# Query parts of the first layer's last piece stacked through DRAM, and every large transfer in pieces on SP's queue

## What is computed

```python
def _L0_xattn_ref(x1, x2, Wq, bq, Wk, bk, Wv, bv, Wo, bo):
    q = _split_heads(x1 @ Wq.T + bq, HEADS)
    k = _split_heads(x2 @ Wk.T + bk, HEADS)
    v = _split_heads(x2 @ Wv.T + bv, HEADS)
    scores = jnp.einsum('bhqd,bhkd->bhqk', q, k) / jnp.sqrt(jnp.float32(dh))
    attn = jax.nn.softmax(scores, axis=-1)
    out = jnp.einsum('bhqk,bhkd->bhqd', attn, v)
    ...
```

## Time and profile before

| | us |
|---|---|
| median of 3 runs (207.86 to 208.6) | 208.3 |
| the profiled execution, its own time | 209.72 |
| its span, first to last instruction | 207.6 |
| PE busy in the span | 192.6 (93%), 1,447 matmuls |
| DVE busy | 144.6 (70%) |
| ACT busy | 141.2 (68%) |
| POOL busy | 65.4 (31%) |
| mean granted TensorE clock | 0.969 |

### The profile page before, as it was taken

The page is one execution under the profiler, slowest core; times in us unless marked ns, Lnnn a source line. Parts: engine busy times, 40 slices in busy tenths (PEclk is TensorE's granted clock), DMA queues, the critical chain, the costliest instruction groups (busy, mean ns, idle before and its releaser), DMA issues.

```text
span 207.6 us, 3929 instructions
## 1 busy us (share of the span) xinstructions
PE 192.6 (93%) x1447; PEld 108.0 (52%) x1454; DVE 144.6 (70%) x222; ACT 141.2 (68%) x262; POOL 65.4 (31%) x91
## 2 busy tenths in 40 slices
PE   7899999699999999896999999989999999999992
PEld 3654566455644643433563545544476656656530
DVE  0499898379968714458756789996867475975661
ACT  2766847847879998835665999798989737341230
POOL 7938894095410000381980000130000032120220
PEclk9999999979999999999579999999999999999997
DMA  6961417440191010085036110011000354005521
GB/s 182 327 266 4 153 3 150 59 152 4 3 201 6 0 6 0 0 278 203 1 75 129 6 1 4 1 5 1 1 4 2 96 188 130 0 6 169 195 95 52
DMA packets 26227, 16.39 MB, mean 79 GB/s; under 512 B 20064, under 2 KB 21776, under 8 KB 26064
## 3 DMA queue, kind: packets, MB, share of 16 engines
q0 software_dynamic: 2528, 9.04, 14.4%
q1 hardware_dynamic: 22672, 6.30, 14.3%
q10 hardware_dynamic: 1008, 0.80, 1.3%
HBM read 13.05 MB, written 3.21 MB: 78 GB/s over the span
## 4 chain that ended last, share of the span: by engine, by line
PE 62%; DVE 11%; ACT 8%; DMA 7%; POOL 6%; SPq 3%; issue 2%; DVEq 0%; POOLq 0%; ACTq 0%
PE PS L398 45%; PE OB L398 17%; DVE T L1143 5%; DMA K<-k_rows 4%; ACT P L991 3%; DMA Q<-T 3%; SPq L723 3%; POOL w_con L785 1%; POOL mix_a L783 1%; POOL mix_b L783 1%; DVE prod_t L1248 1%; POOL k_rows L875 1%; POOL K L890 1%; DVE x L1172 1%; DVE k_lo L1093 1%
## 5 line engine op out<-in xcount | busy, mean ns | idle before, releaser
L1143 DVE TENSOR_REDUCE T<-PS 128x4 fp32r<-128x1024 f32 x64 | 76.2, 1218 | 15.4 <-PE PS L398 15.1
L991 ACT ACTIVATE P<-PS 128x512 f32<-128x512 f32 x128 | 67.8, 607 | 14.3 <-PE PS L398 13.6
L398 PE MATMUL OB<-P,V 128*32 128x256 f32 x512 | 33.7, 392 | 0.0
L398 PEld LDWEIGHTS PS<-K,Q 32*128 32x128 f32 x256 | 19.4, 199 | 23.6 <-issue 8.7
L398 PE MATMUL PS<-K,Q 32*128 32x256 f32 x256 | 29.6, 340 | 2.1 <-DMA K<-k_rows 1.6
L398 PE MATMUL PS<-Q,K 32*128 32x256 f32 x256 | 26.4, 323 | 4.0 <-DMA Q<-T 1.6
L398 PEld LDWEIGHTS PS<-Q,K 32*128 32x128 f32 x256 | 16.8, 185 | 15.2 <-ACT P L991 7.7
L851 POOL TENSOR_TENSOR attn<-o_raw,sums 128x512 f32<-128x512 f32 x4 | 5.1, 1276 | 62.2 <-ACT sums L1020 62.2
L1065 ACT ACTIVATE gate_t<-PS 128x512 f32<-128x512 f32 (+1 forms) x18 | 10.3, 596 | 20.3 <-DVE prod_t L1248 18.2
L861 POOL TENSOR_TENSOR hid_t<-spread,prod_t 128x512 f32<-128x512 f32 x6 | 8.0, 1334 | 50.8 <-PE OB L398 42.7
L398 PEld LDWEIGHTS OB<-P,V 128*32 128x32 f32 x512 | 14.3, 111 | 12.0 <-issue 2.0
(11 more groups left out here) (135 smaller groups left out, 296.3 us busy)
## 6 DMA issues: line engine op xcount, KB each, us to landing
spread<-comb_out SPq DMA_DIRECT2D x32, 128.0 KB, 2.9
K<-k_rows POOLq DMA_DIRECT2D x12, 256.0 KB, 5.0
Q<-T SPq DMA_DIRECT2D x128, 1.0 KB, 2.0
k_rows<-k_hi POOLq DMA_DIRECT2D x6, 256.0 KB, 2.5
w_gu<-gu POOLq DMA_DIRECT2D x1, 1024.0 KB, 6.4
k_rows<-k_lo POOLq DMA_DIRECT2D x3, 256.0 KB, 2.6
w<-w2p POOLq DMA_DIRECT2D x1, 512.0 KB, 6.4
e_up<-eup POOLq DMA_DIRECT2D x1, 508.0 KB, 7.0
```

What stands on the lines that cost most here:

```text
L398: return nc.tensor.matmul(out, lhsT, rhs, start=start, stop=stop)
L991: finish(nc.scalar.activation(P[:, (JOINT * U + j) % (JOINT * PUNITS), :, :].rearrange("p k q -> p (k q)"), PS[:, FILLED["sc", U, j // 2][ ...
L1143: finish(nc.vector.tensor_reduce(T[:, U, 2 * i:2 * i + 2, :], two("max", U, i).rearrange("p j (t s) -> p j t s", t=2), AX.X, ALU.max, nega ...
```

## The change

Query piece (0, 2) joins `MOVED`: its halves are stored and read back through DRAM, as the keys' are. All of `kst`, `kld`, and the new `qst`, `qld` go to SP's queue, each DMA a step of its own (`kst.0.2.2` is one store, `kld.0.2.3` the load of head 3). The load of expert weights goes there too, in four pieces of the gate weights (`ldg`), two of the second weights (`ldw`) and one step of four small ones (`lds`). Each head's loads have a semaphore of their own, so `max.8.0` waits for heads 0 and 1 alone, and `max.8.1` for heads 2 and 3. POOL keeps its arithmetic, and nearly all `hid` steps move from POOL to DVE. The five tables are written anew. PE has four `qsel` steps less (16 for 20) and three fill matmuls more (41 for 38); ACT has 11 `qev` for 16, DVE 5 for 4; DVE has 15 `hid` for 10, POOL 1 for 6.

```diff
-MOVED = ((), ((0, 2), (1, 0), (1, 1)))
+MOVED = (((0, 2),), ((0, 2), (1, 0), (1, 1)))
...
 POOL_ORDER = """
-expand kst.0.2 mixdn kld.0.2 kst.1.0 mixup nmul.0.0 kld.1.0 nmul.0.2 kst.1.1 load wsplit kld.1.1 nmul.1.0
-nmul.1.1 hid.0.2 hid.0.3 hid.0.5 hid.0.6 hid.1.3 hid.1.5
+expand mixdn mixup nmul.0.0 nmul.0.2 nmul.1.0 nmul.1.1 wsplit hid.0.6
 """
 SP_ORDER = """
-ld.1.0 ld.0.0 ld.0.1 ld.1.1 ld.3.0 ld.3.1 ld.2.0 ld.2.1 ld.4.0 ld.5.1 ld.5.0 ld.4.1 ld.6.1 ld.7.0 ld.6.0 ld.7.1
...
+ld.0.1 ld.1.0 ld.0.0 ld.1.1 ld.2.0 kst.0.2.2 ld.2.1 kst.0.2.1 kst.0.2.0 ld.3.1 ld.3.0 ld.4.0 kld.0.2.2
+kld.0.2.1 ld.5.0 qst.0.2.0 qst.0.2.1 qst.0.2.2 ld.4.1 kld.0.2.3 kld.0.2.0 qld.0.2.1 qld.0.2.0 qld.0.2.2
+qld.0.2.3 kst.1.0.0 ld.6.1 ld.5.1 ld.6.0 ld.7.0 ld.7.1 ld.8.1 ld.8.0 ld.10.0 ld.9.1 kst.1.0.1 ld.10.1 ldg.1
...
-        stack_in = [sem(n) for n in ("q_stack_in", "k_stack_in")]
+        stack_in = [[sem(f"{n}_stack_in{j}") for j in range(JOINT)] for n in "qk"]
...
-            return nth(POOL_STEPS, "qld" if kind == 0 else "kld", l, p)
+            kst = "qst" if kind == 0 else "kst"
+            return [s for s in SP_STEPS if s[0] == kst and s[3] == 0].index((kst, l, p, 0)) + 1
...
-        def stacked(eng, kind, l, p, g):
+        def stacked(eng, kind, l, p, g, heads):
 
             if (l, p) in MOVED[kind]:
-                if fresh(eng, stack_in[kind], 64 * move(kind, l, p)):
-                    eng.wait_ge(stack_in[kind], 64 * move(kind, l, p))
+                for j in heads:
+                    if fresh(eng, stack_in[kind][j], 16 * move(kind, l, p)):
+                        eng.wait_ge(stack_in[kind][j], 16 * move(kind, l, p))
...
-                        stacked(pe, kind, l, p, g)
+                        stacked(pe, kind, l, p, g, (2 * i, 2 * i + 1))
...
+                    if fresh(pe, w2_in, 2 * 16):
+                        pe.wait_ge(w2_in, 2 * 16)
...
-            steps = {"ld": turn}
+            def store_part(kind, l, p, r):
+
+                lo, hi = SPANS[l][p]
+                n = move(kind, l, p)
+                low = r == (2 if kind == 0 else 1)
+                after(sp, ("q" if kind == 0 else "k") + ("lo" if low else "hi"), l, p)
+                if n > 1:
+                    for j in range(JOINT):
+                        if fresh(sp, stack_in[kind][j], 16 * (n - 1)):
+                            sp.wait_ge(stack_in[kind][j], 16 * (n - 1))
+                at = slice(0, CH) if kind == 0 else slice(lo, hi)
+                part = ((q_hi, q_lo) if kind == 0 else (k_hi, k_lo))[low]
+                sp.dma_start(part_rows[kind][r + 1], part[:, at].bitcast(f32)).then_inc(parts_out[kind], 16)
+
+            def load_stack(kind, l, p, j):
+
+                lo, hi = SPANS[l][p]
+                n = move(kind, l, p)
+                if fresh(sp, planes_in, 16 * sum(map(bool, MOVED))):
+                    sp.wait_ge(planes_in, 16 * sum(map(bool, MOVED)))
+                if fresh(sp, parts_out[kind], 48 * n):
+                    sp.wait_ge(parts_out[kind], 48 * n)
+                if kind == 0 and l:
+                    if fresh(sp, pv_done, GROUPS * hi // SEQ):
+                        sp.wait_ge(pv_done, GROUPS * hi // SEQ)
+                by_head = part_rows[kind].rearrange("r (d g j) n -> (r d) g j n", g=GROUPS, j=JOINT)
+                sp.dma_start((Q if kind == 0 else K[l])[32 * j:32 * j + 32, :, lo:hi].bitcast(f32), by_head[:, :, j, :])\
+                    .then_inc(stack_in[kind][j], 16)
+
+            def experts_place():
+
+                after(sp, "fwr", 3)
+                after(sp, "fwr", 2)
+
+            def load_gates(q):
+                experts_place()
+                pairs = slice(2 * q, 2 * q + 2)
+                sp.dma_start(w_gu[:, pairs, :, :], gu[:, pairs, :, :]).then_inc(gu_in, 16)
+
+            def load_second(q):
+                experts_place()
+                pairs = slice(4 * q, 4 * q + 4)
+                sp.dma_start(w_2[:, pairs, :], w2p[:, pairs, :]).then_inc(w2_in, 16)
+
+            def load_small():
+                experts_place()
+                for dst, src in ((w_gus[:, :], gus), (w_2s[INTER:D, :], w2s), (w_g[:, :], gwT),
+                                 (gbb[:, :], gate_b.partition_broadcast(D))):
+                    sp.dma_start(dst, src).then_inc(moe_in, 16)
+
+            steps = {"ld": turn, "ldg": load_gates, "ldw": load_second, "lds": load_small,
+                     "qst": lambda *a: store_part(0, *a), "kst": lambda *a: store_part(1, *a),
+                     "qld": lambda *a: load_stack(0, *a), "kld": lambda *a: load_stack(1, *a)}
...
-            def load_experts():
-
-                after(pool, "fwr", 3)
-                after(pool, "fwr", 2)
-                for dst, src in ((w_gu[:, :, :, :], gu), (w_2[:, :, :], w2p),
-                                 (w_gus[:, :], gus), (w_2s[INTER:D, :], w2s),
-                                 (w_g[:, :], gwT),
-                                 (gbb[:, :], gate_b.partition_broadcast(D))):
-                    pool.dma_start(dst, src).then_inc(moe_in, 16)
-
             def split_experts():
 
-                if fresh(pool, moe_in, 6 * 16):
-                    pool.wait_ge(moe_in, 6 * 16)
+                if fresh(pool, gu_in, 4 * 16):
+                    pool.wait_ge(gu_in, 4 * 16)
...
-            def store_parts(kind, l, p):
...
-            def load_stacks(kind, l, p):
...
-            steps = {"qst": store_queries, "kst": store_keys, "qld": load_queries, "kld": load_keys,
-                     "ulo": low_rows, "hid": hidden, "expand": expand, "mixdn": mix_down, "mixup": mix_up, "load": load_experts, "wsplit": split_experts, "nmul": normalise}
+            steps = {"ulo": low_rows, "hid": hidden, "expand": expand, "mixdn": mix_down, "mixup": mix_up, "wsplit": split_experts, "nmul": normalise}```

**SP in the first layer.** Before, SP has nothing but the rows of maxima (Q<-T) after its start-up loads:

```order
L712 DMA w_qk<-wqk 128x512
L714 DMA k_rows<-planes 16x4096
L723 DMA Q<-T 1x128x2 x128
L731 DMA comb_out<-comb_t 16x512
```

182 lines of the change are left out of this document (76 added, 106 removed).

## The result

The changed kernel takes **211.1 us** (median of 19 runs, 210.0 to 217.2) where the kernel before took 208.1 in the same rounds (19 runs, 205.7 to 213.1): a ratio of 1.016, with a 95% interval of 1.012 to 1.020. It is slower by about 1.6%. The forecast was 203.9 with a range to 209.8, and the likeliest side was wrong. The profiled execution of the changed kernel is its slowest, 217.2 us with a span of 215.4; it is read for where the time lies, not for how much there is in the median: by the granted clock, half speed took 8.6 us of it, and 6.1 us of the median execution. 1.5 us of it come before unit 0 is reduced (its x landed later; four experiments that do the same there began on time), and are no part of the change.

A forecast was written before the change was run, and what follows sets the result against it. PE's matmul stream was taken to bound the kernel, except where waits cut it and the clock falls behind them. Terms -0.3 + 0 + 0 - 4.1 = -4.4 us took the median from 208.3 to 203.9, range 200.3 to 209.8.

The forecast's parts named there:

- What bounds the kernel: Whole kernel: PE's matmul stream bounds it, except at cuts, each paid in idle time and then half clock.
- The first wait: At unit 8, keys come sooner and queries by DRAM at 39.0 and 41.4 us: 0, between -3.4 and +3.0.
- The upper bound: At unit 8: +3.0 us, from two key pieces ahead of the queries (2 x 1.2) and 0.6.
- Four `qsel`: On PE before unit 8: four steps of 0.33 us removed, three of them ahead of a wait: -0.3 us.
- SP's queue: 38 DMAs more, 23 us of issue; in units 0 to 7, 8.4 us asked and 4.7 free: cost taken 0.
- Where the layers meet: Before `up.1`: n_hi and n_lo sooner, unit 16's row sooner, seven fills, no clock fall: -4.1 us, 3.4 of it clock.
- The rule weighed there: At the layers' meeting: engines alternate queues by packet, rings keep order; rows still at 4.1 us would cut 1.1 us.
- Layer 2 and the experts: From 107 us on: fewer ACT evictions, more DVE work, `wsplit` ending near 148 under cover: 0, within 1 us.
- Rival 3: First layer, units 0 to 7: SP's queue sets the pace, unit 5's scores 6.2 us late: +1.8, 210.1 us; chance 0.21.
- Rival 1: Behind the layers' meeting: the clock falls all the same, total -2.0, 206.3 us; chance 0.19.
- Rival 4: Between 107 and 150 us: the 4.4 us gained are lost again, ACT perhaps setting the pace: 208.3 us; chance 0.09.

The follow-up runs named there:

- the whole part at the meeting: Kernel before with expert weights in pieces on SP's queue, n_hi ahead of unit 16's first exponential, one query eviction on DVE, seven fills: 205.9 us, ratio 0.996.
- the run placed anew: Changed kernel with piece (0, 2)'s query parts on PE, placed where banks free sooner, and layer 2's pieces ahead of unit 16's rows: 205.6 us, ratio 0.991.

## Why the prediction was wrong

**What bounds the kernel** was read rightly, and the price of a cut, idle time and then clock, was the right one to look for. It was used for the gain and not for the loss.

**The first wait: this is the step that failed.** It was taken as 0, between -3.4 and +3.0. Measured between the two profiled executions, it is +9.6 us with the `qsel`, of which 4.2 waiting and up to 6.8 clock. The experiment in which the queries alone change way, 211.4 against 205.6 us, puts it at 5.7 us in the medians. Laid on one time axis (the start of after taken off, 1.5 us), the queries of heads 0 and 1 were forecast for 39.0 and landed at 43.0; those of heads 2 and 3 for 41.4 and landed at 47.2. Three things were missed:

1. *The issue.* The forecast let the loads start when the stores had landed, 34.7. The stores had landed at 36.64 (35.2 on that axis), and the loads were issued from 37.55 (36.1), behind three stores, two rows and two key loads, one of which took 1.46 us to issue: 0.5 us late by the stores and 0.9 by the queue's turn. The queue's order stood in the diff; the time of the issue was not built from it.
2. *The landing.* Four loads were costed at 1.85 + 4 x 1.2 = 6.7 us. From the first issue to the last landing it was 11.1 us, while two key loads and a store shared the queue: seven transfers of 256 KB. The three other executions with the same transfers took 8.5 to 10.3, so this is the larger miss of the two in every one of them. The upper bound had put the two key loads in, at 2.4.
3. *The clock behind it.* The bound of +3.0 was idle time alone. The earlier trace rows had shown that 1.7 us of idle time brought 1.7 us of clock; two waits brought 8.5 in the profiled execution, and no case of the forecast held this. That is what carried the result past the end of the range. The fills show it: with PE kept busy through both waits, the clock's share goes from 6.1 to 0.3 us and the median to 208.2.

**Four `qsel`** (-0.3): right that most of them lay in a wait. **SP's queue** (0): right for units 0 to 7 in the changed kernel, whose own PE order had moved work ahead; with the old order the rows come late (2.17 us). Wrong in layer 2, where rows behind pieces cost 1.9 us before unit 24, 1.3 of which came back when the pieces were moved. The row there took 4.77 us.

**Where the layers meet** (-4.1): measured -4.1, with `up.1` 6.9 us behind unit 16's first reduction (forecast some 7), and a clock of 1.00 behind it. Between the two profiled executions the size was right, and one reason was not: the sum gave n_hi and n_lo their own share. The run with the expert pieces alone has 7.2 us with n_hi in its old place, and moving it shortened nothing (8.2 us in both runs that did it to a kernel with the row on time; 203.7 us against 203.5). So 2.7 of the 3.0 us were the row that opens unit 16. In the medians the term is too large: 3.4 of its 4.1 us were the clock of one execution, and the expert pieces alone gave 1.7 us, the whole part at the meeting 2.3. The changed kernel with its queries on PE takes 205.6 us, 1.7 above the forecast, which fits this.

**The rule weighed there**, ring order and taking turns between queues. In POOL's transfers' company rows took 4.1 us and up to 7.7 before, and 6.5 and 7.0 in two experiments; a store took 7.86. The first half of the rule (Trainium skill, DMA: Bandwidth & Descriptors, Queues, rings and completion order) says that a DMA engine takes turns between queues. The forecast had drawn from it that another queue's load would delay a row of 1 KB by little; the page gives no such figure, and it is this inference that the rows go against. The second half, order within one ring, agrees with the rows at 66.16 (3.08 us) and 123.93 (4.77 us), both behind pieces on their own queue. But rows beside another queue's loads were as late or later, so no run here tells the order in the ring from the load on the DMA engines.

**Layer 2 and the experts** (0 within 1): `wsplit` started at 147.67 and ended at 155.4, before the first gate at 161.7; it hid, as forecast, though it ended 7 us later than forecast, since the rest was as late (POOL's timeline):

```profile
147.67 0.61 POOL L886 CAST w_hi<-w_gu 128x512 fp32r<-128x512 f32 x1
...
154.10 1.27 POOL L887 TENSOR_TENSOR w_lo<-w_gu,w_hi 128x512 fp32r<-128x512 f32 x1
```

**The rivals.** Rival 3 gave 210.1, near the 211.1 measured, by another mechanism: it held the scores of unit 5 up for rows, and PE's waits were for queries. Half of its premise, a queue without pause, is what delayed the loads' issue by 0.9 us. The other half did not occur: SP came to `qld` at 37.55, after the stores had landed. Of the signs named, one misled: rows of maxima were to land in 2 to 3.5 us, and those behind the query loads took up to 7.6, though PE did not wait for them there. Rival 1 did not occur where it was placed, but where it was not, behind the first wait. Rival 4 did not occur: what the meeting of the layers gained stayed gained, but for the 1.9 us. The chances gave "slower" 0.21; the case that came, queries later than the upper bound with the clock behind them, had none.

## What to carry to other kernels

Whoever moves work from a busy engine to a store and a load on a queue must build the time of that load from the queue's order: each issue ahead of it, the landing of the store, and every transfer that shares the DMA engines, not from one transfer's mean. If the moved work was 1.3 us of an engine and its result is waited for, the way there must be shorter than the slack in front of the wait, else the wait is paid in idle time and again in clock. Large transfers are worth cutting and placing where the queue is idle: the same pieces in the same queue gave 211.1 us between the rows and 204.9 in the gaps, part of it the clock; and where PE must wait, fills in the wait keep the clock, if they end by the time the data land: in one run they held PE back by 2.2 us.

## What was not expected of the hardware

- A half-clock stretch can last much longer than the wait in front of it: 17.1 us behind waits of 3.5 and 2.4 us, 9 of them without any idle time of PE. It is not set by the idle time alone: with one wait of 2.0 us the clock was at half for 17 us, with three stops under 0.8 us for 10 us, and in the run placed anew, busy 3.40 of the 4 us from 41 us on where that one was busy 3.31, not at all. Why these differ stays open; no run told it apart.
- A 256 KB query store took 2.8 us from issue to landing in the changed kernel (median of three), and one took 7.86 us beside four key loads of POOL's queue.
- SP needs about 0.6 us to issue a 256 KB load into 32 partitions, but needed 1.46 us for one of them (36.05 in the chain).
- The same order of transfers on one queue took 8.5, 8.8, 10.3 and 11.1 us from the first of four loads to the last landing in four kernels' profiled executions. Why it varies was not tested.
